# Two helper jobs moved behind the tables' sums, and one alternation of bank pairs for the taps and x's second stage

## The reference, cut to what matters

```python
K  = 2 * real(einsum('hn,hnl->hl', Ct, exp(dtA[:, :, None] * l)))   # 64 modes, 1024 taps per channel
y  = irfft(rfft(x, 2048) * rfft(K, 2048))[:1024]                    # long convolution
x1 = LN(x + LN(x + y + x * D) * ln_w + ln_b)
x2 = LN(x1 + attention(x1, ctx, ctx))                               # 16 heads, 77 keys and values
x3 = LN(x2 + silu(x2 @ Wg + bg) * (x2 @ Wu + bu) @ Wd + bd + product_key_experts(x2))
```

## Time and profile before

| | before |
|---|---|
| median of 3 runs (lowest, highest) | 693.98 us (689.98, 695.78) |
| the profiled execution | 689.71 us, of which the span is 687.9 us |
| PE, DVE, ACT, POOL busy | 87%, 70%, 59%, 45% of the span |
| TensorE's mean granted clock | 0.92 of full speed |
| PE matmul busy, by fortieths of the span | 6809588795769598999999999999999999899896 |

### The profile page before, as it was taken

One profiled execution on the slowest core, in us unless ns is written; L12 is line 12 of the kernel. 1 busy time (PEld: TensorE's weight loads), 2 busy tenths in 40 slices (PEclk: granted clock), 3 DMA queues, 4 the chain that ended last, 5 costly groups with the idle time before them and its releaser, 6 DMA issues.

```text
span 687.9 us, 9791 instructions
## 1 busy us (share of the span) xinstructions
PE 599.0 (87%) x3200; PEld 393.4 (57%) x3200; DVE 484.3 (70%) x955; ACT 403.9 (59%) x595; POOL 308.5 (45%) x354
## 2 busy tenths in 40 slices
PE   6809588795769598999999999999999999899896
PEld 2503477573636364454776745578565478453485
DVE  7976475662346885897857789765779796678782
ACT  3865446222143265996673878773778774677760
POOL 3704975554142456352263632243735243744441
PEclk9858879899695677999999999999999999999999
DMA  8994020368161000000000000000000000000000
GB/s 272 309 235 90 1 76 27 101 171 224 27 247 59 1 1 1 0 2 0 1 0 1 17 8 9 0 1 1 8 16 1 9 1 1 9 15 9 0 9 23
DMA packets 19613, 34.14 MB, mean 50 GB/s; under 512 B 7273, under 2 KB 13931, under 8 KB 18219
## 3 DMA queue, kind: packets, MB, share of 16 engines
q1 hardware_dynamic: 15179, 29.33, 14.8%
q10 hardware_dynamic: 4384, 4.20, 1.9%
HBM read 21.81 MB, written 10.65 MB: 47 GB/s over the span
## 4 chain that ended last, share of the span: by engine, by line
PE 64%; DVE 12%; DMA 6%; ACT 6%; POOL 6%; issue 5%; SPq 1%; DVEq 0%; POOLq 0%; ACTq 0%
PE banks L804 20%; PE banks L894 8%; PE banks L899 8%; PE banks L849 4%; PE banks L871 4%; PE banks L826 3%; DMA scr_x<-arena 3%; PE banks L861 3%; PE banks L679 2%; PE banks L746 2%; PE banks L835 2%; DMA scr_v<-arena 2%; PE banks L886 2%; DVE stats L1437 2%; PE banks L716 1%
## 5 line engine op out<-in xcount | busy, mean ns | idle before, releaser
L1260 POOL TENSOR_TENSOR arena<-arena 128x1024 f32<-128x1024 f32 x64 | 123.3, 1927 | 159.1 <-ACT arena L1122 158.3
L804 PE MATMUL banks<-arena 128*128 128x512 f32 x384 | 174.4, 596 | 5.3 <-issue 3.7
L804 PEld LDWEIGHTS banks<-arena 128*128 128x128 f32 x384 | 69.8, 190 | 83.0 <-issue 76.9
L1122 ACT ACTIVATE arena<-arena 128x1024 f32<-128x1024 f32 x64 | 73.5, 1149 | 7.5 <-DVE arena L1525 3.0
L1124 ACT ACTIVATE arena<-arena 128x1024 f32<-128x1024 f32 x64 | 73.5, 1149 | 2.1
L1525 DVE SCALAR_TENSOR_TENSOR arena<-arena 128x1024 f32<-128x1024 f32 x48 | 63.9, 1331 | 1.7
L1012 ACT COPY arena<-banks 128x512 f32<-128x512 f32 (+1 forms) x64 | 34.1, 532 | 46.2 <-PE banks L796 30.3
L894 PE MATMUL banks<-arena 128*128 128x256 f32 x256 | 58.4, 381 | 2.4 <-DVE arena L1547 2.2
L1233 POOL TENSOR_SCALAR arena<-mv 128x1 f32<-128x1 f32 (+1 forms) x40 | 14.4, 361 | 102.1 <-DVE mv L1438 100.7
L899 PE MATMUL banks<-arena 128*128 128x256 f32 x256 | 57.9, 379 | 0.0
L1026 ACT ACTIVATE tok<-tok,arena,rstd 128x256 f32<-128x256 f32 x48 | 27.9, 598 | 44.0 <-POOL arena L1238 43.0
(11 more groups left out here) (179 smaller groups left out, 1096.3 us busy)
## 6 DMA issues: line engine op xcount, KB each, us to landing
scr_x<-arena SPq DMA_DIRECT2D x16, 256.0 KB, 8.9
arena<-scr_x SPq DMA_DIRECT2D x4, 1024.0 KB, 11.0
scr_z<-arena ACTq DMA_DIRECT2D x14, 256.0 KB, 3.8
tok<-in_x SPq DMA_DIRECT2D x8, 256.0 KB, 6.1
arena<-scr_z SPq DMA_DIRECT2D x4, 512.0 KB
out<-tok SPq DMA_DIRECT2D x16, 128.0 KB, 1.7
arena<-scr_z SPq DMA_DIRECT2D x2, 640.0 KB
arena<-in_imat SPq DMA_DIRECT2D x1, 1152.0 KB, 5.5
```

Of the source, the lines that this page charges most:

```text
L804: ins = mm(bk[:, :], w[:, k, P * m:P * m + P], src[:, k, :], start=(k == 0), stop=(k == KC - 1))
L1122: fn(ebuf[m % 2], sxb[m % 2], ACT.Prelu, bias=negt[:, n % 2, h:h + 1], alpha=FAR).then_inc(s_ranked, 1)
L1260: tt(sxb[m % 2], sim[:, n % 2, h, 0:XR].unsqueeze(2).broadcast_to((P, XR, NKEYS)), sim[:, n % 2, FH + h, :].unsqueeze(1).broadcast_to((P, ...
```

## The change

Three things change.

1. **Due times.** `values` goes from -1.576 to 7.2 and `x_bias` from about -0.5 to 12, so on POOL the values stand behind all the tables' sums and the residual biases behind all spectra. `keys` goes from 9.738 to 7.6: on DVE it stands between the last tables and the first spectra. `stage` and `simw` swap, and both stand behind the second set of sines on ACT. `x_second` goes from (-2.2, 0.237) to (-0.5, 0.77), so that the steps of x's second stage are spread between the taps.
2. **Banks.** Taps and x's second stage now share one alternation: each such step takes the pair that the step before it didn't take, in PE's order, and waits until ACT has copied out the step two places ahead of it.
3. Many other due times move in the fourth digit. On PE and on ACT `turno` 2 moves up one place, past `ln` 7, which issues nothing there; the order of instructions there stays. Three `k_first`/`inverse` steps of the second half move by one place.

```diff
-         "taps": (0.982,), "x_second": (-2.2, 0.237), "skip": (1.3, 0.3), "k_first": (5.915, 0.66, 9.6, 0.247),
-         "simw": (-2.4,), "x_bias": (-0.466, 0.617), "values": (-1.576,), "stage": (-2.515,), "keys": (9.738,),
+         "taps": (0.982,), "x_second": (-0.5, 0.77), "skip": (1.3, 0.3), "k_first": (5.915, 0.66, 9.6, 0.247),
+         "simw": (-2.284,), "x_bias": (12.0, 0.1), "values": (7.2,), "stage": (-1.936,), "keys": (7.6,),
...
+        PAIR_USERS = [y for y in order(HEAD, "pe") if y[0] in ("taps", "x_second")]
+        PAIR_AT = {y: i for i, y in enumerate(PAIR_USERS)}
...
-        def x_bank(m):
-
-            return 4 * (m % 2)
-
-        def group_bank(g):
-
-            return 4 * (g % 2)
+        def pair_bank(kind, n):
+
+            return 4 * ((PAIR_AT[kind, n] + 1) % 2)
+
+        def pair_free(kind, n):
+
+            at = PAIR_AT[kind, n]
+            if at < 2:
+                return (s_xae, 2 * NQ) if at else (s_kbz, 1)
+            last, k = PAIR_USERS[at - 2]
+            return (s_kev, 2 * k + 2) if last == "taps" else (s_xfe, k + 1)
...
-                if g >= 2:
-                    pe.wait_ge(s_kev, 2 * g - 2)
-                b0 = group_bank(g)
+                pe.wait_ge(*pair_free("taps", g))
+                b0 = pair_bank("taps", g)
...
-                b0 = x_bank(k1)
-                if k1 > 1:
-                    pe.wait_ge(s_xfe, k1 - 1)
-                elif k1 == 1:
-                    pe.wait_ge(s_kbz, 1)
+                pe.wait_ge(*pair_free("x_second", k1))
+                b0 = pair_bank("x_second", k1)
...
-                    if n == 0:
-                        pe.wait_ge(s_kbz, 1)
-                        pe.wait_ge(s_xfe, FREQ)
```

More of the change, by code:

```diff
@@ L55 @@
 PAIRS = [(0, NC)] + [(2 * m - 1, 2 * m) for m in range(1, FREQ - 1)] + [(NC - 1,)]
[L58 to L64, removed]
+PLACE = {"probs": (0.166, 0.2592, 0.441), "score": (0.273, 0.6341), "attend": (0.592,), "turno": (0.772,),
+         "project": (1.4,), "project_last": (0.934,), "turn1": (-0.087, 0.0432), "query": (0.245, 0.2685),
+         "turn2": (-0.001, 0.0655), "sim": (0.379,), "sim_first": (0.031,), "best": (0.432,), "best_first": (0.207,),
+         "pair": (0.283, 0.3903, 0.7922, 0.8026), "total": (0.847,), "first": (-0.1,), "sums": (-0.805,),
+         "exps": (-0.131,), "late": (-0.027, 0.0082, 0.7012),
+         "conv": (-2.338, -1.7115, -1.497, -1.4195, -1.329, -1.2905, -1.172, -0.9595),
+         "ln": (-1.672, -1.4035, 0.316, 1.2245, 1.9406, 2.373, 3.035, 3.1435),
@@ L65 @@
          "ln_steps": (-0.409, -0.234, 0.162, 0.013, 0.361), "sines": (-2.943, -2.336), "tables": (0.152,),
-         "taps": (0.982,), "x_second": (-2.2, 0.237), "skip": (1.3, 0.3), "k_first": (5.915, 0.66, 9.6, 0.247),
-         "simw": (-2.4,), "x_bias": (-0.466, 0.617), "values": (-1.576,), "stage": (-2.515,), "keys": (9.738,),
-         "diagonal": (-1.42,), "k_second": (8.773, 0.13, 9.955, 0.1), "spectra": (9.027, 0.13, 10.11, 0.1),
+         "taps": (0.982,), "x_second": (-0.5, 0.77), "skip": (1.3, 0.3), "k_first": (5.915, 0.66, 9.6, 0.247),
@@ L69 @@
+         "simw": (-2.284,), "x_bias": (12.0, 0.1), "values": (7.2,), "stage": (-1.936,), "keys": (7.6,),
+         "diagonal": (-0.992,), "k_second": (8.773, 0.13, 10.002, 0.1), "spectra": (9.027, 0.13, 10.11, 0.1),
          "inverse": (9.103, 0.13, 10.25, 0.11), "products": (0.0, 1.0, 0.0, 0.996, 0.0, 0.802, -0.084, 0.975),
-         "probs_alone": (0.016, 0.079, 0.473), "score_alone": (0.367, 0.6874), "attend_alone": (0.566,),
+         "probs_alone": (0.016, 0.0791, 0.4732), "score_alone": (0.367, 0.6875), "attend_alone": (0.566,),
@@ L910, in evac_taps @@
             g, half = divmod(i, 2)
-            src = bank[group_bank(g) + half][:, :].rearrange("p (k c) -> p c k", c=P)
+            src = bank[pair_bank("taps", g) + half][:, :].rearrange("p (k c) -> p c k", c=P)
             ch = CH * (g % HALF_GROUPS) + HC // 2 * half
@@ L985, in _ @@
                     r, m = tiles_of(n)[0], rows_of_pair(n)
-                    own.link(nc.scalar.copy(xS[m, r, :], bank[x_bank(n)][m, :]))
-                    nc.scalar.copy(xS[m, image_of(n), :], bank[x_bank(n) + 1][m, :]).then_inc(s_xfe, 1)
+                    own.link(nc.scalar.copy(xS[m, r, :], bank[pair_bank("x_second", n)][m, :]))
+                    nc.scalar.copy(xS[m, image_of(n), :], bank[pair_bank("x_second", n) + 1][m, :]).then_inc(s_xfe, 1)
                     own.done(s_xfe)
```

## The result

The changed kernel takes 676.26 us (median of 4, 674.96 to 677.25) against 694.05 us of the kernel before (median of 4). The medians lie 17.8 us apart. The ratio of the comparison is not that of the two medians; it is 0.9762, with a 95% interval from 0.9728 to 0.9797, which is 16.5 us of 694.05; 16.0 was forecast (678.0, range 671 to 687). In a later comparison the same kernel took 676.79 us against 690.37, 0.9794 (0.9762 to 0.9827). The profiled executions differ by less, 14.0 us in the span (673.9 after 687.9), and by parts not quite as forecast, which most of what follows is about.

A forecast was written before the change was run, and what follows sets the result against it. The head was taken to be bound by POOL's wait for the values and PE's x steps ahead of taps 0; -15.4 us (ladder) and -0.6 (keys) make -16.0, so 678.0 us against 693.98, range 671 to 687.

The forecast's parts named there:

- What bounds the kernel: In the head, POOL's wait for the values and PE's nine x steps delay taps 0; DVE waits 15.05 us.
- The start: Earlier sines on ACT start DVE's tables at 51.2; behind two x steps, taps 0 begin at 57.0 instead of 71.7.
- First term: Ladder of taps, x steps and copies: taps 7 end at 104.0 instead of 119.45, a gain of 15.4 us.
- hand-overs: In the path to taps 7, about a dozen passings between engines were allowed 0.1 us each.
- Two signs of the prediction's own list: DVE's longest wait before tables 2 below 1 us; taps 7 waiting for POOL's sum beside the keys would show it wrong.
- rival B: TensorE's clock at 0.83 in the ladder takes 8.4 us of the gain, giving 686.4 us; chance 0.15.
- rival C: PE and ACT alternate without overlap in the ladder: taps 7 end at 115, gain 4.5, 689.5 us; chance 0.06.
- Rival D: TensorE's clock stays at 0.5 in the ladder: about 20 us late, 714 us; chance 0.03.
- second term: Keys leave the spectra for DVE's idle time, saving PE's wait: -0.6 us, with POOL's last sum beside them costing 0.
- the worst reading: DVE's port lock makes POOL stand for all four keys, some 3.2 us; the sum loses 2.2 us of gain.
- Values and biases: On POOL, 2.7 us and 9.9 us of work fit into idle time; biases end 8.6 us early, cost 0.
- Sum: Whole kernel: -15.4 - 0.6 = -16.0 us, a span of 671.9 after 687.9, median forecast 678.0.

The follow-up runs named there:

- e1: The kernel before with only the values and residual biases moved behind POOL's other work; 685.86 us, ratio 0.9915.
- e2: The changed kernel with all steps of x's second stage put back ahead of all taps; 683.0 us, ratio 0.9874.
- e3: The changed kernel with values and residual biases back at their early places on POOL; 694.34 us, ratio 1.0035.
- e6: The changed kernel with stage and simw back between the two sets of sines on ACT; 676.32 us in one execution.
- e8: The changed kernel with the two halves of the taps alternating from matmul to matmul; 671.88 us, ratio 0.9748.
- e7: The changed kernel with only the residual biases back at their early places on POOL; 682.91 us, ratio 0.9887.
- e10: The changed kernel with taps' halves in turn, the eighth x step behind taps 4 and the keys behind all spectra; 679.12 us, ratio 0.9833.
- e4: The changed kernel with the keys back between the spectra of the first half on DVE; 677.96 us, ratio 0.9784.

## Why the prediction was right, point by point

- **What bounds the kernel: right.** e1, e2 and e3 show the two obstacles in a row: POOL's alone taken away is worth 4.2 us (7.7 with the rest of the change), the x steps' alone -2.0, both 14.5. That the new alternation of banks gains something even without the spread (e2 against e1) is not in the prediction.
- **The start: right, and partly for nothing.** DVE's tables began at 50.15 instead of 51.2. Taps 0 began 5.9 us behind x0, as the sum had it (50.98 to 57.0). The earlier sines, which the working lists at length, are worth 0.4 us at most (e6), since PE's x steps end later than POOL's first sum either way.
- **First term: the step that was mis-sized.** Taps 7 end at 107.1 and not at 104.0, -12.4 us and not -15.4. Four terms of the working were too small. x0 began 1.1 us later on its transfer. The two groups of 64 records took 5.04 us each, where the 2.13 us of the others had been doubled: 1.5 in all; e8 shows that the runs of four cost it. The last x step was put at 0.9, half of the others, for its half as many matmuls, but it takes as long as they do (1.93 against 1.94): 1.0. And PE waits 0.61 us for the last sum of v. That makes 4.2 against the 3.1 measured; the 1.2 us allowed for hand-overs were mostly not needed. Two signs of the prediction's own list went against it: DVE's wait before tables 2 is 2.90 us and not below 1 (taps 0 end 1.7 us later than forecast and DVE is ready 1.0 us earlier), and taps 7 do wait for POOL's sum beside the keys.
- **The clock (rival B): refuted for this kernel.** The granted clock was 1.00 over the whole of 57 to 104, through waits of 0.6 to 1.5 us. Longer waits did cost it in the experiments: behind 3.01 us (e7) and 5.95 us (e1, e2) the taps took 7.86 us for 64 records and 3.92 for 32, where 5.04 and 2.13 are full speed, with a granted clock of 0.50, the lower level (1.2 GHz), in e7 and e2. Behind 1.92 us in e1 taps 4 took 6.56 at 0.74 on the mean, and behind the 3.48 us in e10 the last x step took 3.64 instead of 1.93. B's sum has a slip: by the prediction's own durations the taps are 21.4 us of PE's work (6 x 2.13 + 2 x 4.3) and not 21.8; its 8.4 us stay as good as they were.
- **PE and ACT strictly in turn (rival C): no.** ACT was busy for 25 of the 34 us from 70 to 104. Rival D did not come near.
- **Keys: the new place was priced wrongly.** The second term was -0.6. The spectra's part became 1.05 us shorter, of which the keys are 0.60 (e4 against the changed kernel), as forecast; no run shows where the other 0.45 come from. But the keys' 0.60 were given back by their collision with POOL's sum at the new place: e4 finds 0.05 us in all. I had costed that collision at 0 since the sum would be ready ahead of `k_first` 3; it was ready 0.6 us too late. The size of the collision was right: 2.92 instead of 2.35, where "about 0.6" stood. The traces refute the worst reading, POOL blocked for all four keys, some 3.2 us. All four places of the keys show delays of 0.4 to 0.6 us for each sum on POOL, and 4.1 to 6.1 us for the keys' own four. The Trainium skill ("SBUF — State Buffer", SBUF: two separate sides) has an exclusive lock, held for the whole instruction, for such pairs; one instruction waiting for one of the other engine, in turns, agrees with these rows.
- **Values and biases: right.** The values cost nothing, though stretched from 2.72 to 4.08 us beside the keys; the biases end 10.3 us ahead of the first deviation (8.6 forecast).
- **Sum: right in total, in part by luck.** By the two traces: -12.4 to taps 7, -1.05 to the last inverse, +1.7 on z's way, -2.3 in the rest, -14.0 where -16.0 was forecast. The last two stood at nothing in the prediction, and traces of kernels with the same code there differ by as much. By the ratio (0.9762) the change is worth 16.5 us, by the stretch that it edits 14.5. The difference of 2 us lies within the interval of the ratio (14.1 to 18.9 us) and stays open. So the mechanism is shown, but the first term was 3.1 us too large, and that the total came nearer to the forecast than that term is luck.

## What to carry to other kernels

When an engine that works in order stands before a chain, look for every obstacle before pricing one: here POOL's wait and PE's nine steps ended within a microsecond of each other, and removing either alone was worth about half at the most, or less than nothing. Work that only has to be done sometime belongs into the waits of a chain that alternates between engines: it no longer delays the chain's start, and it keeps PE from standing idle long enough to lose its clock. Where two series share a ring of buffers, exchanging two steps changes whom they and the steps behind them wait for, so each step's partner must be read off anew. A hole in one engine's time is no free place if what is put there slows an engine that is on the path, as the keys slowed POOL's sums.

## What the runs showed of the hardware that I had not expected

- Matmuls of 64 rows and 128 columns that alternate between the upper and the lower half of the array's rows, and between two banks, go through at 0.060 us a record (3.84 / 64, e8; each matmul is two records). In runs of four on one half and one bank they took 0.079 (5.04 / 64), in runs of two 0.067 (2.13 / 32), against 0.064 (2.05 / 32) when those groups alternate.
- x's second stage: four matmuls of 512 columns that alternate between the two halves of a bank's rows took 1.94 us, and the two matmuls of the last step, which write one half alone, 1.93 us. The second half came free.
- The keys' four instructions of 128 x 616 on DVE took 4.1 us beside short sums on POOL (0.73 us alone) and 5.4 to 6.1 beside long ones (2.35 us alone), where in the chain of the kernel before the first and the last of the four took 0.81 each: the longer the instruction on POOL, the longer DVE stands.
